# The last stage of a Mamba block with a ternary feed-forward gate: the second matmul in two half passes, with its bias added on TensorE

## The reference

```python
xn  = layernorm(x)
fwd = mamba(xn, weights_f);  bwd = flip(mamba(flip(xn), weights_b))
s   = concatenate([fwd, bwd], -1) @ wproj.T + bproj          # [2048, 2048] @ [2048, 1024]
h   = relu(xn @ quantize(W1).T + b1)                         # [2048, 4096]
g   = silu(h @ quantize(W2).T + b2)                          # [2048, 4096] @ [4096, 1024]
out = x + s * g
```

## Time and profile before

| | us |
|---|---|
| median of three runs | 6594.18 |
| the profiled execution's own time | 6599.41 |
| its span, slowest core (core 4) | 6597.9 |
| cores' spans | 6565.3 to 6597.9 |
| third part, first load to last instruction (core 4) | 6015.1 to 6597.9 |

### The profile page before, as it was taken

How to read it: one execution, slowest core, us unless ns; L and a number is a source line. 1 busy time by engine, 2 the same in 40 slices (tenths; PEclk the granted TensorE clock), 3 DMA queues, 4 the chain that set the end, 5 groups by cost and what they waited for, 6 DMA issues and landing times. The chain is left out here.

```text
span 6597.9 us, 36375 instructions; the slowest of 8 cores (6565.3 to 6597.9 us)
## 1 busy us (share of the span) xinstructions
PE 2802.2 (42%) x8066; PEld 925.1 (14%) x8066; DVE 4697.0 (71%) x5351; ACT 2121.5 (32%) x3486; POOL 470.0 (7%) x846
## 2 busy tenths in 40 slices
PE   2053333433343334333444445444544443334677
PEld 1010011111111001011111111111111111111222
DVE  3327888688858884888588876888588858981111
ACT  3013334333333333333343343333333333330000
POOL 0100000000000000000000000000000000001111
PEclk9965555655565556555666667666666675557999
DMA  6521111111111111111121111111111110004222
GB/s 193 150 46 46 23 23 24 47 23 24 23 48 24 23 27 46 23 24 24 50 56 35 33 36 51 32 37 32 52 32 37 32 47 23 24 21 106 74 81 90
DMA packets 150869, 303.30 MB, mean 46 GB/s; under 512 B 54384, under 2 KB 71424, under 8 KB 147584
## 3 DMA queue, kind: packets, MB, share of 16 engines
q0 software_dynamic: 86960, 241.80, 15.6%
q1 hardware_dynamic: 63696, 59.18, 2.9%
HBM read 331.35 MB, written 50.59 MB: 58 GB/s over the span
## 5 line engine op out<-in xcount | busy, mean ns | idle before, releaser
L732 ACT ACTIVATE dA_sl<-delta_sb,A_sb 128x512 bf16<-128x512 bf16 x2048 | 1309.1, 710 | 2509.0 <-DVE h_sl L784 2094.2
L799 PE MATMUL py<-h_sl,ident 128*128 128x512 bf16 x2048 | 909.1, 595 | 2618.6 <-DVE h_sl L784 2065.1
L758 DVE TENSOR_TENSOR_SCAN h_sl<-dA_sl,hcar,dBu_sb 128x512 bf16<-128x512 bf16 x1024 | 1231.6, 1265 | 27.6 <-DVE dBu_sb L747 1.4
L765 DVE TENSOR_TENSOR_SCAN h_sl<-dA_sl,hcar,dBu_sb 128x512 bf16<-128x512 bf16 x1024 | 1231.6, 1265 | 27.3 <-DVE dBu_sb L747 0.9
L747 DVE TENSOR_TENSOR dBu_sb<-du_sb,B_bc 128x2048 bf16<-128x2048 bf16 x512 | 625.2, 1221 | 331.5 <-ACT dA_sl L732 290.6
L799 PEld LDWEIGHTS py<-h_sl,ident 128*128 128x128 bf16 x2048 | 231.2, 127 | 3243.5 <-issue 3228.8
L535 PE MATMUL pdb<-xn_cm,wslot 128*128 128x512 bf16 x1024 | 438.3, 605 | 559.5 <-DMA wslot<-win_sl_f 273.8
L784 DVE TENSOR_TENSOR h_sl<-h_sl,C_bc 128x2048 bf16<-128x2048 bf16 x512 | 627.3, 1225 | 55.9 <-DVE hcar L775 4.5
L446 PE MATMUL pw<-xn_cm,w1f 128*128 128x512 bf16 x1024 | 405.4, 567 | 0.0
L535 PE MATMUL px<-xn_cm,wslot 128*128 128x512 bf16 x1024 | 331.4, 483 | 45.9 <-DMA wslot<-win_sl_f 45.9
L1029 DVE TENSOR_TENSOR gstage<-px,b2bc 128x512 bf16<-128x512 f32 x8 | 5.2, 686 | 445.4 <-PE pw L1013 445.4
(11 more groups left out here) (117 smaller groups left out, 2631.8 us busy)
## 6 DMA issues: line engine op xcount, KB each, us to landing
wslot<-win_sl_f POOLq DMA_DIRECT2D x128, 256.0 KB, 4.0
wslot<-win_sl_b POOLq DMA_DIRECT2D x128, 256.0 KB, 3.7
xst<-x SPq DMA_DIRECT2D x32, 512.0 KB, 3.8
wstg<-w1t_sl POOLq DMA_DIRECT2D x8, 2048.0 KB, 9.9
wstg<-w2t_sl POOLq DMA_DIRECT2D x32, 512.0 KB, 3.6
B_bc<-bc_scr POOLq DMA_DIRECT2D x8, 2048.0 KB, 8.0
C_bc<-bc_scr POOLq DMA_DIRECT2D x8, 2048.0 KB, 12.7
qst<-w1t_sl POOLq DMA_DIRECT2D x64, 256.0 KB, 3.8
```

The costliest lines, as they stand in the source:

```text
L732: e.activation(out=o, in_=i, func=AF.Exp, scale=sc),
L758: e.tensor_tensor_scan(out=o, data0=d0, data1=d1, initial=i, op0=ALU.mult, op1=ALU.add),
L765: e.tensor_tensor_scan(out=o[:, ::-1], data0=d0[:, ::-1], data1=d1[:, ::-1], initial=i, op0=ALU.mult, op1=ALU.add),
L799: e.matmul(out=o, lhsT=ident[:], rhs=r, start=st, stop=sp), sPE if last else None)
```

## The change

All of it is in the third part.

1. The W2 matmul of a chunk is done in two passes over the 32 slices, with 4 banks each: pass 0 does token tiles 0 and 1 in `pdb`, `py0`, `py1`, `pw`; pass 1 does tiles 2 and 3 in `px0`, `px1`, `pd0`, `pd1`. Each load brings 256 tokens of a slice in place of 512, into one of two slots that each pass has for itself, so there are 64 loads of half the size to a chunk.
2. The biases are no longer repeated over partitions. `b2r_sb` and `bpr_sb` hold one row each. A float32 matmul of `ones34` (one row of 128 ones) by 512 entries of that row starts each bank's accumulation, in place of the first real matmul: 8 for b2 and 8 for bproj in a chunk.
3. ScalarE applies Silu to the banks directly. VectorE's addition into `gstage` is gone, and so is its addition of `bpbc`: the multiplication by g reads the bank.
4. Waits: pass 0 waits for ScalarE's Silus of the chunk before and not for VectorE; pass 1 waits for VectorE's last two tiles of the chunk before. TensorE's very first matmul of this part waits for all loads of biases and `wproj_sb`. A projection half waits for the Silu of its bank.

```diff
-            b2bc = p34.enter_context(nc.sbuf_tensor("b2bc", [P, D], F32))
-            bpbc = p34.enter_context(nc.sbuf_tensor("bpbc", [P, D], F32))
+            ones34 = p34.enter_context(nc.sbuf_tensor("ones34", [1, P], F32))
+            b2r_sb = p34.enter_context(nc.sbuf_tensor("b2r_sb", [1, D], F32))
+            bpr_sb = p34.enter_context(nc.sbuf_tensor("bpr_sb", [1, D], F32))
...
+            PASSES = [([pdb, py[0], py[1], pw], [(0, 0), (0, 1), (1, 0), (1, 1)],
+                       sH1G),
+                      ([px[0], px[1], pd[0], pd[1]],
+                       [(2, 0), (2, 1), (3, 0), (3, 1)], sH1G2)]
             for c in range(NCH):
                 t0 = c * TC
-                if c > 0:
-                    b.wait("tensor", sV, pj_out[4 * c - 1])
-                for ft in range(NFT):
...
+                for ps, (banks, tiles, sems) in enumerate(PASSES):
+                    if ps == 0:
+                        for i4, (tt, hf) in enumerate(tiles):
+                            pv = gsil.get((c - 1, tt, hf))
+                            if pv:
+                                b.wait("tensor", sA, pv)
+                    else:
+                        if c > 0:
+                            b.wait("tensor", sV, pj_out[4 * (c - 1) + 2])
+                            b.wait("tensor", sV, pj_out[4 * (c - 1) + 3])
+                    if c == 0 and ps == 0:
+                        b.wait("tensor", sV, v_on)
+                        b.wait("tensor", sBulkG, v_wp)
+                    for i4, (tt, hf) in enumerate(tiles):
+                        b.op("tensor", lambda e, o=banks[i4][:],
+                             w=ones34[0:1, 0:P],
+                             r=b2r_sb[0:1, hf * TC:(hf + 1) * TC]:
+                             e.matmul(out=o, lhsT=w, rhs=r, start=True, stop=False))
+                    for ft in range(NFT):
+                        par = ft % 2
+                        prev = h1mm.get((c, ps, ft - 2)) or \
+                               (h1mm.get((c - 1, ps, NFT - 2 + ft))
+                                if ft < 2 and c > 0 else None)
+                        if prev:
+                            b.wait("gpsimd", sPE, prev)
+                        vh = b.dma("gpsimd", sems[par],
+                                   h1sl[:, (ps * 2 + par) * HB:
+                                        (ps * 2 + par + 1) * HB],
+                                   h1_scr[ft][:, t0 + ps * 2 * P:
+                                              t0 + ps * 2 * P + 2 * P])
+                        b.wait("tensor", sems[par], vh)
...
-                        vv = b.op("vector", lambda e, o=gsl, pb=bank,
-                                  bb=b2bc[:, hf * TC:(hf + 1) * TC]:
-                                  e.tensor_add(out=o, in0=pb[:], in1=bb), sV)
...
+                            pb=banks[i4]:
+                            e.activation(out=o, in_=pb[:], func=AF.Silu), sA)
...
-                        b.wait("tensor", sV, gev01[(c, pjbidx[hf])])
+                        b.wait("tensor", sA, gsil[(c, pjtt, hf)])
+                        b.op("tensor", lambda e, o=bank[:], w=ones34[0:1, 0:P],
+                             r=bpr_sb[0:1, hf * TC:(hf + 1) * TC]:
+                             e.matmul(out=o, lhsT=w, rhs=r, start=True, stop=False))
...
-                        v_a = b.op("vector", lambda e, o=ssl, pb=bank,
-                                   bb=bpbc[:, hf * TC:(hf + 1) * TC]:
-                                   e.tensor_add(out=o, in0=pb[:], in1=bb), sV)
-                        b.wait("vector", sV, v_a)
-                        v_m = b.op("vector", lambda e, o=ssl, a1=ssl,
-                                   a2=g_sb[:, tl * D + hf * TC:tl * D + (hf + 1) * TC]:
-                                   e.tensor_mul(out=o, in0=a1, in1=a2), sV)
+                        v_m = b.op("vector", lambda e, o=ssl, pb=bank,
+                                   a2=g_sb[:, tl * D + hf * TC:
+                                           tl * D + (hf + 1) * TC]:
+                                   e.tensor_mul(out=o, in0=pb[:], in1=a2), sV)
```

More of the change, by code:

```diff
@@ L138, in build_program @@
         sH1G = [Sem(nc, ctx, f"sH1G{i}") for i in range(2)]
+        sH1G2 = [Sem(nc, ctx, f"sH1G2{i}") for i in range(2)]
         xn = ctx.enter_context(nc.sbuf_tensor("xn_cm", [P, NKD * T], BF16))
@@ L957, in build_program @@
             sstage = p34.enter_context(nc.sbuf_tensor("sstage", [P, 2 * TC], BF16))
[L959 to L962, removed]
+            v_on = b.op("vector", lambda e: e.memset(ones34[:], 1.0), sV)
+            b.dma("gpsimd", sBulkG, b2r_sb[:], dr["b2row"])
+            b.dma("gpsimd", sBulkG, bpr_sb[:], dr["bprojrow"])
             for jj in range(NKD):
@@ L974, in build_program @@
                 w2half.append(v)
+            HB = TC // 2
             h1mm = {}
[L977 removed]
             gsil = {}
@@ L981, in build_program @@
             pj_st = {}
-            gev01 = {}
+            PASSES = [([pdb, py[0], py[1], pw], [(0, 0), (0, 1), (1, 0), (1, 1)],
+                       sH1G),
+                      ([px[0], px[1], pd[0], pd[1]],
+                       [(2, 0), (2, 1), (3, 0), (3, 1)], sH1G2)]
             for c in range(NCH):
                 t0 = c * TC
-                if c > 0:
-                    b.wait("tensor", sV, pj_out[4 * c - 1])
-                for ft in range(NFT):
[L988 to L1009, removed]
@@ new lines, in build_program @@
+                for ps, (banks, tiles, sems) in enumerate(PASSES):
[29 more added lines that the diff above has]
+                        b.wait("tensor", sems[par], vh)
+                        if c == 0 and ps == 0:
+                            b.wait("tensor", sW2s[ft // (NFT // 2)],
+                                   w2half[ft // (NFT // 2)])
+                        for i4, (tt, hf) in enumerate(tiles):
+                            last = (i4 == 3)
+                            v = b.op("tensor", lambda e, o=banks[i4][:],
+                                     w=h1sl[:, (ps * 2 + par) * HB
+                                            + (tt - 2 * ps) * P:
+                                            (ps * 2 + par) * HB
+                                            + (tt - 2 * ps + 1) * P],
@@ L1010, in build_program @@
                                      r=w2q_sb[:, ft * D + hf * TC:
                                               ft * D + (hf + 1) * TC],
-                                     st=(ft == 0), sp=(ft == NFT - 1):
-                                     e.matmul(out=o, lhsT=w, rhs=r, start=st,
+                                     sp=(ft == NFT - 1):
+                                     e.matmul(out=o, lhsT=w, rhs=r, start=False,
                                               stop=sp), sPE if last else None)
-                    h1mm[(c, ft)] = v
@@ L1016, in build_program @@
[L1016 to L1026, removed]
-                        vv = b.op("vector", lambda e, o=gsl, pb=bank,
-                                  bb=b2bc[:, hf * TC:(hf + 1) * TC]:
-                                  e.tensor_add(out=o, in0=pb[:], in1=bb), sV)
-                        if 2 * tt + hf in (0, 1, 3, 4):
-                            gev01[(c, 2 * tt + hf)] = vv
-                        b.wait("scalar", sV, vv)
+                        h1mm[(c, ps, ft)] = v
@@ L1033, in build_program @@
+                    b.wait("scalar", sPE, v)
+                    for i4, (tt, hf) in enumerate(tiles):
+                        if c > 0:
+                            b.wait("scalar", sV, pj_out[4 * (c - 1) + tt])
                         gsil[(c, tt, hf)] = b.op("scalar", lambda e,
-                            o=g_sb[:, tt * D + hf * TC:tt * D + (hf + 1) * TC], i=gsl:
-                            e.activation(out=o, in_=i, func=AF.Silu), sA)
+                            o=g_sb[:, tt * D + hf * TC:tt * D + (hf + 1) * TC],
+                            pb=banks[i4]:
+                            e.activation(out=o, in_=pb[:], func=AF.Silu), sA)
@@ L1066, in build_program @@
                                                 k * D + (hf + 1) * TC],
-                                     st=(k == 0), sp=last:
-                                     e.matmul(out=o, lhsT=w, rhs=r, start=st, stop=sp),
+                                     st=False, sp=last:
+                                     e.matmul(out=o, lhsT=w, rhs=r, start=st,
+                                              stop=sp),
                                      sPE if last else None)
```

3 lines of the change are left out of this document (1 added, 2 removed).

## The result

The changed kernel takes 6865.88 us, the median of 8 runs (6848.31 to 6886.82), against 6596.75 us for the kernel before (8 runs). The ratio is 1.0405, with a 95% interval of 1.0388 to 1.0423: 4.1% slower. The forecast was 6896 us, slower, in a range of 6790 to 6990 us. The profiled execution took 6858.0 us with a span of 6856.1 us on its slowest core, core 6.

The account below looks back on a forecast made before the run. TensorE was taken to wait repeatedly for small h1sl loads in the third part. 265 + 56 - 14 - 5 - 4 + 4 = +302 us on 6594 gave 6896 us, 4.6% slower, range 6790 to 6990 us.

Parts of the forecast that it names:

- The passes: W2 matmuls in the third part: eight passes of 76.5 us, 612 us against 347, so +265 us.
- The refill: Time to refill a slot between its bursts in a pass: taken as 3.25 us, against 3.35 us before.
- the 6 us a pass that I allowed for late loads: Added to each W2 pass's 70.5 us for loads that land late, giving 76.5 us.
- The clock: TensorE's clock in the passes swings between levels: 70.5 us a pass, the middle of 63.4 and 77.7.
- held: Rival: idle stretches split evenly, 1.2 us each, and the clock in the passes stays at 1.00; 6824 us, chance 0.22.
- low: Rival: the clock in the passes stays at its lower level; 6992 us, chance 0.12.
- The bias matmuls: TensorE's float32 bias matmuls for b2 and bproj: 56 on the path at 1.0 us each, +56 us.
- the rival of two full-price instructions: Rival: each float32 bias matmul costs 1.7 to 3.5 us, +95 to +196 us; about 6960 us, chance 0.08.
- a few at the lower clock: Allowance within the 1.0 us per bias matmul, above 0.86 us at 2.4 GHz.
- 24 - 14 - 5 + 4 = +9 us: Projection: 24 bproj matmuls, less VectorE wait (-14) and shorter VectorE work (-5), plus less cover for its first load (+4).
- The first loads: Start of the third part, bandwidth-bound: two bias tiles of 0.5 MB fall away, -4 us.
- Faster through four slots: Rival: pass 1's loads run ahead during pass 0, so the four slots hide the loads; 6505 us, chance 0.02.

Follow-up runs that it names:

- e1: Changed kernel with one pass over the slices on all 8 banks instead of two, VectorE wait back at a chunk's start: 6661.64 us, ratio 1.0106.
- e3: Changed kernel with four slots for each pass in place of two: 6580.90 us, ratio 0.9985 to the kernel before.
- e4: Changed kernel with every W2 matmul of the passes issued twice, same slots, loads and waits: 6929.03 us, ratio 1.0513.
- e2: Changed kernel with the ones and both bias rows in bf16 instead of float32: 6797.29 us, ratio 1.0310.
- e9: Kernel of e1 with ones and bias rows as float32 tiles of 128 partitions, zero below row 0: 6624.70 us, ratio 1.0048.
- e7: Changed kernel with eight slots for each pass and bias matmuls in bf16: 6462.70 us, ratio 0.9803.
- e5: Kernel before the change with four slots of h1sl in place of two, nothing else changed: 6473.32 us, ratio 0.9819.
- e10: Kernel of e7 with ones and bias rows as tiles of 128 partitions, zero below row 0: 6473.08 us, ratio 0.9794.
- e6: Changed kernel with each pass loading 512 tokens of a slice and using half: 6940.06 us, ratio 1.0527.
- e8: Kernel of e1 with four slots and bias matmuls in bf16: 6492.35 us, ratio 0.9829.

## Why the prediction was right, step by step

- **The whole.** The forecast was 6896 us, and 6865.88 were measured. Part of the closeness is luck: the passes came out 54 us too high, the bias matmuls of b2 9 us and the projections 11 us too low, and these misses cancel in part.
- **The passes, +265 forecast, +211 measured.** The mechanism is shown by e1 (take the split back: -204 us), e3 (hide the latency with slots: -285 us) and e4 (double the work: only +63 us). The size was 54 us too high in two terms. The refill is 3.09 us, not 3.25: 8 x 15 x 0.16 = 19 us. The estimate of 3.1 us that the prediction made from the Trainium skill's fixed part of about 2.0 us (DMA: Bandwidth & Descriptors, Anatomy of one DMA) came closer. The trace agrees with it: the landing went from 2.5 to 2.2 us. The other 35 us are the 6 us a pass that I allowed for late loads: with a refill of 3.09 us, halfway between the clocks, a pass comes to 15 x 4.37 + 2.6 = 68 us, and 69.8 us were measured, so under 2 us were needed. At the full clock the same sum gives 15 x 3.95 + 1.7 = 61 us: of the 211 us some 70 are an estimate of what the lower clock costs on this core, and the rest is the turns.
- **The clock.** That it would swing between its levels was right: 0.71 to 0.79 in all passes of the slowest core, and 0.75 to 0.95 on core 7. Both rivals on it, held and low, fall. But the picture behind it was wrong. The prediction had the bursts of the two slots standing together, with an idle stretch of 2.4 us in every turn like the late load's 2.14 us. The trace has them apart, with stretches of about 1 us, which is the picture of the rival in which the clock holds; and with those it fell. So the right level was in part luck. What the runs show in its place is that the length of the burst matters at the same refill (e4); at which pattern the clock tips stays open.
- **The bias matmuls, +56 forecast.** At the full clock one costs 0.9 us, as read from the transposes, and the rival of two full-price instructions falls. But b2's 32 took 40.7 us in place of 32, and e2 gives 69 us for all 64. The term that was too small is "a few at the lower clock". Before each pass 0 of chunks 1 to 3 the four take 3.6 to 3.8 us at clock 1.00, but before each pass 1 they take 5.2 to 6.3 us at 0.59 to 0.67, for they follow a pass in which the clock swings; in e3, behind a dense pass, the same four take 3.6 us. Longer runs of them also let the clock fall by themselves (e1 against e9).
- **The projection.** I had 24 - 14 - 5 + 4 = +9 us, and it was +19.8. The wait at a chunk's start is gone: pass 0's bias matmuls begin at 6255.7, where the last projection matmul ends. The price of bproj's matmuls is not the main part of the miss of 11 us: in bf16 (e2) the projections are 18.8 us shorter, and 24 matmuls at 0.7 us less would be 17. They are then at 186.1 us, where 185.1 were before, while the forecast's relief of 15 us and 24 matmuls at 0.25 us would give 176. The means of the eight cores say the same: 185.6 us before, 187.0 in e2 and 207.8 in the changed kernel. So it is mostly relief that is missing, and where it is lost was not told apart.
- **The first loads, -4 forecast:** -4.6 us, 45.7 in place of 50.3.
- **Faster through four slots:** fell as forecast, since two slots a pass wait for their own pass. That four slots a pass do it is e3.

## What to carry to other kernels

Where an engine waits for a small load into a slot that it has itself to free, the turn is burst plus latency: halving the work per turn halves what is hidden and leaves the latency. Count slots against (burst + refill) / burst before splitting a loop: here that is 2.9 in the kernel before and 4.6 in a pass, with two slots in both. Four slots alone turned the loss of 4.1% into a gain of 0.15% (e3), and eight slots with bf16 biases into one of 2.0% (e7); two more slots gave 1.8% without the split or any other part of the change (e5). A bias as a matmul is not free on a bound TensorE: take bf16 if the precision allows (e2). In float32 and eight in a row, filling all 128 rows with zeros was faster as well (e9); in bf16 and four in a row no gain was measured (e10).

## What the runs showed of the hardware that was not expected

- Float32 matmuls with one row of the array did not raise the clock. In e1, 12.0 us of them with no gap ran at granted clock 0.50, and with 128 rows (e9) the same instructions ran at 0.70 to 1.00 and the kernel was 37 us faster. A short run of them did no harm to a clock that was up: four took 3.6 us at 1.00.
- Idle stretches of about 1 us between bursts of 4 matmuls were enough for the clock to swing, 0.71 to 0.79 on core 6 of the changed kernel, and the same passes ran at 0.75 to 0.95 on core 7.
- In the execution of e10 the granted clock stood at 0.81 for long stretches, between the two levels, with TensorE nearly always busy. Core 0, three windows, then one pass of core 1 (PE busy, PEclk, DMA share, GB/s):

```profile
6060.00:6120.00 60.00, 58.81 (x222) 0.81 0.29 84
6160.00:6220.00 60.00, 59.55 (x225) 0.81 0.23 70
6355.00:6410.00 55.00, 54.74 (x245) 0.98 0.34 97
```
```profile
6093.10:6126.90 33.80, 33.79 (x129) 0.81 0.36 88
```

  In the third part the cores of e10 had this level for 64 to 248 us each. It is not special to e10 or to its chip: the trace of the kernel before has it on cores 4 to 7, for 72 to 104 us in all, e2's and e7's have it on cores 0 to 3, e6's on cores 4 to 7 and e4's on all, while e8's, from the same chip as e10's, has none. What brings it about, and whether e10's 128-row bias matmuls make it longer, is open.
